# Five orders and their banks written anew, and 24 more unread products

## The reference, cut to what matters

```
mod = (silu(c) @ wmod) -> sa, ca, ga, sb, cb, gb       # per batch, per layer
# layer 0
h = layernorm(x) * (1 + ca) + sa
q, k, v = h @ w_qkv.T ; q, k = elu + 1                 # 16 heads of 8
x = x + ga * ((q @ (k^T v)) / (q @ sum k) @ w_proj.T + b)
h = layernorm(x) * (1 + cb) + sb
x = x + gb * sum over the top 2 of 8 experts: gate * (gelu(h' @ W1 + b1) @ W2 + b2)   # 128 -> 512 -> 128
# layer 1
h = layernorm(x) * (1 + ca) + sa
x = x + ga * softmax(q k^T / 4) v                      # 8 heads of 16, v 128 wide, heads summed
h = layernorm(x) * (1 + cb) + sb
x = x + gb * (h + expert_w[argmax] @ h)                # top 1 of 8
```

## Time and profile before

| | us |
|---|---|
| three runs, median | 690.94 |
| lowest, highest | 690.84, 691.75 |
| the profiled execution | 690.36 |
| its span | 688.6 |
| PE busy | 603.1 (88%) |
| DVE busy | 481.5 (70%) |
| ACT busy | 390.5 (57%) |
| POOL busy | 334.4 (49%) |
| mean granted clock of PE | 0.965 |

### The profile page before, as it was taken

The page is one execution under the profiler, slowest core; times in us unless marked ns, Lnnn a source line. Parts: engine busy times, 40 slices in busy tenths (PEclk is TensorE's granted clock), DMA queues, the critical chain, the costliest instruction groups (busy, mean ns, idle before and its releaser), DMA issues. The chain is left out here.

```text
span 688.6 us, 11893 instructions
## 1 busy us (share of the span) xinstructions
PE 603.1 (88%) x3825; PEld 386.9 (56%) x3825; DVE 481.5 (70%) x1213; ACT 390.5 (57%) x866; POOL 334.4 (49%) x363
## 2 busy tenths in 40 slices
PE   7988996999899888678998999988889897999875
PEld 4656555988798787566426498632243424533232
DVE  5277885456374654478866862896999773889996
ACT  2543043697676656336887766767665565664420
POOL 5222185447347863552773441454756273157423
PEclk9998998999999989989999999999999999999997
DMA  8200124577589688497637687216130627411121
GB/s 337 105 0 1 58 113 153 169 250 239 206 259 343 200 293 271 125 319 227 230 117 209 202 286 245 86 41 178 54 70 1 176 76 189 150 47 35 28 61 31
DMA packets 47037, 106.40 MB, mean 155 GB/s; under 512 B 7056, under 2 KB 22224, under 8 KB 45440
## 3 DMA queue, kind: packets, MB, share of 16 engines
q1 hardware_dynamic: 41424, 94.82, 43.4%
q0 software_dynamic: 5120, 10.50, 4.9%
q10 hardware_dynamic: 432, 0.34, 0.2%
HBM read 80.26 MB, written 25.17 MB: 153 GB/s over the span
## 5 line engine op out<-in xcount | busy, mean ns | idle before, releaser
L894 ACT ACTIVATE bufa<-PS 128x512 f32<-128x512 f32 x256 | 139.4, 599 | 75.2 <-PE PS L1563 68.8
L1205 DVE TENSOR_REDUCE mxs<-PS 128x2 f32<-128x1024 f32 x128 | 151.1, 1219 | 32.1 <-PE PS L1547 31.4
L853 ACT ACTIVATE bufb<-PS,bufb 128x128 f32<-128x128 f32 x368 | 103.3, 380 | 45.0 <-PE PS L1512 44.7
L1512 PE MATMUL PS<-bufb 128*128 128x128 f32 x736 | 97.5, 281 | 14.2 <-DMA bufb<-in_experts_dram 8.4
L1512 PEld LDWEIGHTS PS<-bufb 128*128 128x128 f32 x736 | 91.0, 196 | 21.0 <-issue 9.8
L1520 PE MATMUL PS<-bufb 128*128 128x128 f32 x736 | 96.3, 279 | 0.7 <-ACT bufb L853 0.6
L693 POOL DMA_INDIRECT slots_in<-bufb x64 | 67.5, 1055 | 56.4 <-DVE bufb L1151 38.3
L706 POOL DMA_INDIRECT bufb<-slots_out,bufb x64 | 61.7, 963 | 67.9 <-DMA bufb<-slots_out,bufb 35.5
L1520 PEld LDWEIGHTS PS<-bufb 128*128 128x128 f32 x736 | 90.1, 195 | 4.2 <-ACT bufb L853 1.4
L1547 PE MATMUL PS<-stk 96*128 96x512 bf16 x256 | 74.7, 384 | 15.1 <-DVE mxs L1205 5.3
L1563 PE MATMUL PS<-stk 108*128 108x512 bf16 x256 | 80.8, 387 | 7.9 <-ACT bufa L894 6.8
(11 more groups left out here) (291 smaller groups left out, 968.8 us busy)
## 6 DMA issues: line engine op xcount, KB each, us to landing
bufb<-in_experts_dram SPq DMA_DIRECT2D x92, 514.0 KB, 4.8
stk<-split SPq DMA_DIRECT2D x48, 256.0 KB, 5.2
slots_out<-bufb SPq DMA_DIRECT2D x30, 256.0 KB, 4.1
bufb<-slots_in SPq DMA_DIRECT2D x25, 256.0 KB, 3.0
split<-terms SPq DMA_DIRECT2D x8, 768.0 KB, 3.8
slots_in<-hb SPq DMA_DIRECT2D x2, 1536.0 KB, 9.5
X<-in_x_dram SPq DMA_DIRECT2D x4, 512.0 KB, 6.5
out_dram<-X SPq DMA_DIRECT2D x6, 256.0 KB, 3.4
```

The lines of the kernel that those rows point to most:

```text
L853: last = nc.scalar.activation(hs[:, n % HR, fc, :], ps[:, P * fc:P * fc + P], ACT.Gelu_apprx_tanh, bias=ws[:, n % WR, F + fc:F + fc + 1])
L894: nc.scalar.activation(probs[:, i % PR, j, :], psum("s2", i, j), ACT.Exp, scale=DH1 ** -0.5)\
L1205: nc.vector.tensor_reduce(mxs[:, gr % 2, 2 * j:2 * j + 2, h], psum("s1", i, j).rearrange("p (c n) -> p c n", c=2), axis=AX.X, op=ALU.max)\
L1512: last = nc.tensor.matmul(ps[:, P * fc:P * fc + P], ws[:, n % WR, P * fc:P * fc + P], xq[:, q % 2, P * x:P * x + P], start=True, stop=True)
```

## The change

Only the five texts of ORDERS are changed. In PE's 801 items at least 253 stand elsewhere (by 14 places at most), in ACT's 499 at least 131, in DVE's 332 at least 60, in POOL's 95 at least 15, in SP's 183 at least 47. Of 669 items with a bank 347 have another. The unread products in the loop go from 170 at 21 items to 194 at 33: two new ones at each of anm.3.1, bh.1.11, bxt.1.4, bh.2.0, bh.2.2, ctr.0.0, bh.2.5, bxt.2.2, bh.2.7, cpv.0.0, s1.1.0 and mt.0.0 ("~5"); the old ones keep their counts. ldv.0.0 moves by 76 places and is nothing still. The lines that the prediction speaks of, cut:

```diff
 "PE"
-        pc.0.0@0 atr.0.0@1 pm.0.0@0~38 aq.0.0@0~18 akv.0.0@1 akv.0.1@0 akx.0.0@0~31 anm.0.0@1~5 anm.0.1@0 aot.0.0@1~23
+        pc.0.0@1 pm.0.0@1~38 atr.0.0@1 aq.0.0@0~18 akv.0.0@1 akv.0.1@0 akx.0.0@1~31 anm.0.0@1~5 anm.0.1@0 aot.0.0@0~23
...
-        bh.1.21@2 bh.1.22@1 by.1.20@2 bxt.2.0@0 by.1.21 bxt.2.1@1 bh.2.0@0 by.1.22 btr.3.0@1 bh.2.1@0 by.2.0@1 bh.2.2@2 bh.2.3@0
-        by.2.1 ctr.0.0@0 bh.2.4@2 by.2.2 by.2.3 blg.3.0@1 bh.2.5@2 bh.2.6@0 bxt.2.2@2 by.2.4@1 by.2.5 bh.2.7@2 cpq.0.0@0
-        bh.2.8@0 bh.2.9@2~7 by.2.6 by.2.7 cpv.0.0@1 bxt.2.3@1 bh.2.10@2 bgt.3.0@0 by.2.8@1 by.2.9 bh.2.11@0 bh.2.12@2 by.2.10
-        bh.2.13@0 by.2.11 bgb.3.0@0 cpq.1.0@1 bh.2.14@1 bh.2.15@2 by.2.12@0 cpv.1.0@0 by.2.13 by.2.14 s1.0.0@0 s1.0.1@1
+        by.1.19 by.1.20@0 by.1.21 by.1.22 bxt.2.0@2 bh.2.0@2~5 bh.2.1@1 bh.2.2@2~5 ctr.0.0@0~5 bxt.2.1@0 by.2.0@2 btr.3.0@1
+        bh.2.3@1 by.2.1 by.2.2 by.2.3 bh.2.4@1 bh.2.5@1~5 cpq.0.0@1 bh.2.6@0 bxt.2.2@2~5 bh.2.7@0~5 by.2.4@2 blg.3.0@0
+        bh.2.8@0 cpv.0.0@0~5 by.2.5 by.2.6 bh.2.9@0~7 bh.2.10@1 by.2.7 cpq.1.0@0 bxt.2.3@0 bgt.3.0@2 by.2.8@1 by.2.9
+        by.2.10 bh.2.11@0 bh.2.12@2 bgb.3.0@1 by.2.11 by.2.12@0 bh.2.13@1 bh.2.14@2 bh.2.15@1 by.2.13 by.2.14 bxt.2.4@1
+        bxt.2.5@2 s1.0.0@0 cpv.1.0@1 by.2.15 s1.0.1@0 s1.1.0@0~5 bh.2.16@1 s1.1.1@1 bh.2.17@0 bh.2.18@1 s1.2.0@0 by.2.16@0
 "ACT"
-        atr.0.0 aw.0.0 aw.1.0 pm.0.0 aw.2.0 aq.0.0 akv.0.0 akv.0.1 aot.0.0 pm.0.1 aw.3.0 pm.1.0 pm.1.1 aw.4.0 pr.0.0 atr.1.0
+        aw.0.0 pm.0.0 atr.0.0 aw.1.0 aq.0.0 akv.0.0 aw.2.0 akv.0.1 aot.0.0 pm.0.1 pm.1.0 aw.3.0 aw.4.0 atr.1.0 pm.1.1
...
-        bxt.2.0 bh.2.0 by.1.5 bxt.2.1 bh.2.1 btr.3.0 bh.2.2 bh.2.3 ctr.0.0 bh.2.4 by.2.0 bh.2.5 bxt.2.2 bh.2.6 bh.2.7 cpq.0.0
-        blg.3.0 by.2.1 bh.2.9 bxt.2.3 bh.2.8 bgt.3.0 bh.2.10 bh.2.11 bh.2.12 bh.2.13 by.2.2 cpq.1.0 bh.2.14 bh.2.15 bxt.2.4
+        bh.1.18 bh.1.19 bh.1.17 bh.1.20 bh.1.21 bh.1.22 bxt.2.0 by.1.4 by.1.5 bh.2.0 bh.2.1 bh.2.2 bxt.2.1 bh.2.3
+        btr.3.0 bh.2.4 by.2.0 ctr.0.0 bh.2.6 bh.2.5 bxt.2.2 bh.2.7 cpq.0.0 blg.3.0 bh.2.8 by.2.1 bh.2.9 bh.2.10 cpq.1.0
+        bgt.3.0 bxt.2.3 bh.2.11 bh.2.12 by.2.2 bh.2.13 bh.2.14 bh.2.15 bxt.2.4 bxt.2.5 by.2.3 bh.2.16 bh.2.17 bh.2.18
 "DVE"
-        an1.0.0 an2.0.0 pc.0.0 an1.1.0 aph.0.0 apk.0.0 apk.0.1 akx.0.0 anm.0.0 anm.0.1 apr.0.0 bn1.0.0 an2.1.0 bn2.0.0 bn3.0.0
-        aph.1.0 bn4.0.0 apk.1.0 apk.1.1 an1.2.0 akx.1.0 blm.0.0 anm.1.0 anm.1.1 blg.0.0 bgt.0.0 brk.0.0 apr.1.0 bn1.1.0 an2.2.0
-        bn4.3.0 cn3.0.0 cn4.0.0 bcm.1.0 blm.3.0 blg.3.0 bgt.3.0 cpv.0.0 cpq.0.0 bcm.1.2 bcm.1.1 bcm.1.3 bcb.1.0 cn1.1.0 bgb.3.0
-        mx.15.1 bcm.2.1 msp.3.0 bcm.2.2 cpv.3.0 mtc.3.0 mx.16.0 mx.16.1 bcm.2.3 mx.17.1 bcb.2.0 cn1.2.0 mx.17.0 mx.18.0 mx.18.1
-        ds.2.0 dl2.3.0 rds.1.0 dll.3.0 fil.3.1 dx.3.0 en1.0.1 dy.3.1 dl2.3.1 dx.3.2 dy.3.3 dll.3.1 ds.3.0 dx.3.4 dy.3.5 dx.3.6
+        an1.0.0 pc.0.0 an2.0.0 an1.1.0 aph.0.0 apk.0.0 apk.0.1 akx.0.0 anm.0.0 anm.0.1 apr.0.0 bn1.0.0 an2.1.0 bn2.0.0
+        bn3.0.0 aph.1.0 an1.2.0 bn4.0.0 apk.1.0 apk.1.1 akx.1.0 blm.0.0 anm.1.0 anm.1.1 blg.0.0 bgt.0.0 brk.0.0 apr.1.0
+        cn1.0.0 bn2.3.0 bn3.3.0 bgb.2.0 cn2.0.0 cn3.0.0 bn4.3.0 cn4.0.0 cpq.0.0 blm.3.0 cpv.0.0 blg.3.0 bgt.3.0 bcm.1.0
+        mtc.2.0 mx.12.0 mx.12.1 mx.13.0 cpq.3.0 mx.13.1 mx.14.0 mx.14.1 mx.15.0 mx.15.1 msp.3.0 bcm.2.0 cpv.3.0 mtc.3.0
+        mx.16.0 bcm.2.1 bcm.2.2 mx.16.1 mx.17.0 mx.17.1 bcm.2.3 bcb.2.0 cn1.2.0 mx.18.0 mx.19.0 mx.18.1 cn2.2.0 mx.19.1
+        dx.3.0 en1.0.1 dy.3.1 dl2.3.1 dx.3.2 dy.3.3 dll.3.1 dx.3.4 dy.3.5 dx.3.6 ds.3.0 dy.3.7 ds.3.1""",
 "POOL"
-        bsc.2.2 cn1.0.0 bsc.2.3 bn3.3.0 cn2.0.0 cn3.0.0 bga.1.0 bga.1.1 bga.1.2 bga.1.3 cpt.0.0 cn1.1.0 cn2.1.0 cn3.1.0 cpt.1.0
-        rsc.0.1 rsc.0.2 cpt.7.0 rsc.0.3 fin.2.0 dn1.2.0 rga.0.0 rga.0.1 rga.0.2 rga.0.3 dx.2.0 dx.2.2 dx.2.4 dx.2.6 en1.0.0
+        bn1.3.0 bsc.2.1 bsc.2.2 bsc.2.3 cn1.0.0 bn3.3.0 cn2.0.0 cn3.0.0 bga.1.0 bga.1.1 bga.1.2 cpt.0.0 bga.1.3 cn1.1.0
+        dx.2.0 dx.2.2 dx.2.4 dx.2.6 rga.0.3 en1.0.0 dx.3.0 en1.0.1 dx.3.2 dx.3.4 dx.3.6""",
 "SP"
-        byo.0.2 byo.0.3 bw.0.22 bw.1.0 bw.1.1 byo.0.4 byo.0.5 bxl.1.0 bxl.1.1 bxl.1.2 bw.1.2 bxl.1.3 bxl.1.4 bw.1.3 bw.1.4
-        bw.2.14 cto.0.0 bw.2.15 cst.0.0 bxl.2.4 bxl.2.5 bw.2.16 bw.2.17 bw.2.18 byo.2.1 bw.2.19 bw.2.20 bw.2.21 byo.2.2 cto.1.0
+        bw.0.21 byo.0.2 bw.0.22 bxl.1.0 bxl.1.1 bxl.1.2 bw.1.0 bw.1.1 byo.0.3 byo.0.4 byo.0.5 bw.1.2 bxl.1.3 bw.1.3
+        bxl.2.4 bxl.2.5 bw.2.10 bw.2.11 cto.0.0 bw.2.12 bw.2.13 bw.2.14 bw.2.15 byo.2.0 byo.2.1 cst.0.0 bw.2.16 bw.2.17
```

More of the change, by code:

```diff
@@ L73 @@
[L73 to L81, removed]
@@ L86 @@
[L86 to L94, removed]
@@ L95 @@
[L95 to L111, removed]
-        s2.32.1@1 s2.32.2@0 fin.1.0@1 s2.32.3@0 s2.33.0@2 s2.33.1@1 ctr.3.0@1 s2.33.2@1 fin.1.1@0 pv.8.0 s2.33.3@0 s1.37.1@1
@@ new lines @@
+        pc.0.0@1 pm.0.0@1~38 atr.0.0@1 aq.0.0@0~18 akv.0.0@1 akv.0.1@0 akx.0.0@1~31 anm.0.0@1~5 anm.0.1@0 aot.0.0@0~23
+        apr.0.0@0~10 pm.0.1@1 pm.1.0@1 pm.1.1@1~9 atr.1.0@0~17 aq.1.0@0~18 pr.0.0@1~9 akv.1.0@0 akv.1.1@1 btr.0.0@1~15
+        akx.1.0@0~6 blg.0.0@1 anm.1.0@0 anm.1.1@1 aot.1.0@1~23 brk.0.0@0~30 apr.1.0@1 atr.2.0@1~90 aq.2.0@0~18 bgt.0.0@1
+        akv.2.0@1 akv.2.1@0 bgb.0.0@0 akx.2.0@0~22 anm.2.0@1~5 anm.2.1@0 bxt.0.0@0~15 aot.2.0@1 bh.0.0@1 bh.0.1@2
+        bxt.0.1@1 bh.0.2@2 apr.2.0@1 btr.1.0@0 bh.0.3@0 by.0.0@1 by.0.1 by.0.2 bh.0.4@0 blg.1.0@0 bxt.0.2@2 by.0.3
@@ new lines @@
+        atr.3.0@1 bh.0.5@0 by.0.4@2 bh.0.6@1 bh.0.7@0 bh.0.8@1 by.0.5 by.0.6 by.0.7 bxt.0.3@0 bh.0.9@0 aq.3.0@0
+        bh.0.10@2 bh.0.11@0 brk.1.0@1 bxt.0.4@2 bgt.1.0@0 by.0.8@1 by.0.9 by.0.10 by.0.11 bh.0.12@0 bh.0.13@2 bgb.1.0@0
+        bh.0.14@0 bh.0.15@1 by.0.12@2 bh.0.16@0 bh.0.17@1 by.0.13 by.0.14 by.0.15 bxt.0.5@2 bh.0.18@0 akv.3.0@0
+        by.0.16@0 akv.3.1@1 bh.0.19@2 bh.0.20@1 akx.3.0@0 by.0.17 bh.0.21@1 bh.0.22@2 by.0.18 by.0.19 by.0.20@0 by.0.21
+        by.0.22 anm.3.0@1 anm.3.1@1~5 bxt.1.0@0 bxt.1.1@2 btr.2.0@0 bh.1.0@2 blg.2.0@0 bh.1.1@0 aot.3.0@0 bh.1.2@2
@@ new lines @@
+        pv.3.1 s2.14.2@2 s2.14.3@1 s2.15.0@0 s1.18.0@0 s1.18.1@1 s2.15.1@2 s2.15.2@1 s2.15.3@0 pv.3.2 bh.3.4@1 bh.3.5@0
+        s1.19.0@0 pv.3.3 bh.3.6@2 bh.3.7@1 s1.19.1@1 bh.3.8@0 by.3.4@2 by.3.5 bxt.3.3@0 s1.20.0@0 by.3.6 s1.20.1@1
+        by.3.7 bh.3.9@1 s1.21.0@0 s1.21.1@1 by.3.8@2 bh.3.10@0 by.3.9 bh.3.11@1 mt.4.0@1 by.3.10 s1.22.0@1 bh.3.12@0
+        ctr.2.0@0 by.3.11 bh.3.13@1 cpq.4.0@0 bh.3.14@0 bh.3.15@2 by.3.12@1 by.3.13 s1.22.1@1 bxt.3.4@0 bxt.3.5@2
+        by.3.14 by.3.15 bh.3.16@2 bh.3.17@0 s1.23.0@1 cpq.5.0@0 by.3.16@0 bh.3.18@2 bh.3.19@1 by.3.17 bh.3.20@2
@@ new lines @@
+    "POOL": """
+        an1.0.0 anx.0.0 an1.1.0 bn1.0.0 bn3.0.0 anx.1.0 an1.2.0 bsc.0.0 bn1.1.0 bsc.0.1 bsc.0.2 bsc.0.3 bn3.1.0 anx.2.0
+        an1.3.0 pk.0.0 bn1.2.0 anx.3.0 bsc.1.0 bsc.1.1 bsc.1.2 bsc.1.3 bn3.2.0 bga.0.0 bga.0.1 bga.0.2 bsc.2.0 bga.0.3
+        bn1.3.0 bsc.2.1 bsc.2.2 bsc.2.3 cn1.0.0 bn3.3.0 cn2.0.0 cn3.0.0 bga.1.0 bga.1.1 bga.1.2 cpt.0.0 bga.1.3 cn1.1.0
+        cpt.1.0 cn2.1.0 cn3.1.0 bsc.3.0 bsc.3.1 bsc.3.2 bsc.3.3 bga.2.0 cpt.2.0 bga.2.1 bga.2.2 cpt.3.0 bga.2.3 cn1.2.0
+        cn2.2.0 cn3.2.0 cpt.4.0 bga.3.0 bga.3.1 bga.3.2 bga.3.3 cpt.5.0 cn1.3.0 fin.0.0 cn2.3.0 cn3.3.0 dn1.0.0 dmo.0.0
+        fin.1.0 dn1.1.0 dmo.1.0 cpt.6.0 rsc.0.0 rsc.0.1 rsc.0.2 cpt.7.0 rsc.0.3 fin.2.0 dn1.2.0 rga.0.0 rga.0.1 rga.0.2
+        dx.2.0 dx.2.2 dx.2.4 dx.2.6 rga.0.3 en1.0.0 dx.3.0 en1.0.1 dx.3.2 dx.3.4 dx.3.6""",
```

200 lines of the change are left out of this document (111 added, 89 removed).

## The result

The changed kernel takes 716.92 us (median of 4 runs, 711.65 to 719.77) where the kernel before takes 690.89 (686.50 to 691.75): a ratio of 1.038, interval 1.031 to 1.046. That is 26 us slower and not 5 us faster, 31 us above the forecast of 685.5 and outside its range of 678 to 693. Its profiled execution, the slowest of the four, took 719.77 us with a span of 718.0.

A forecast was written before the change was run, and what follows sets the result against it. It took TensorE and its waits to bound the early stages, TensorE and VectorE in turn the second half. Terms summed to −7.0, cut to −5.0 for overlap: 690.36 to 685.4, taken as 685.5 us; range 678 to 693.

The forecast's parts named there:

- Part 7: Whole kernel: 24 more unread products cost +0.8 us (0 to 5.3); banks and other moves 0, bounds ±2.
- Rival C: Unread products keep no clock, since waits of several us remain, and only delay what follows: about 688.5 us; chance 0.10.
- Part 1: Opening: modulations go first, aq.0.0 starts 3.2 us earlier; net −1.0 us at the first scatter, bounds −2.5 and 0.
- Part 2: Loads of pair 1: TensorE's 1.79 us idle at 184.32 goes as bxl.1.0 is issued earlier; −1.8 us, or 0.
- Part 3: 235 to 256 us: 4.59 us of idle becomes about 7 at ctr.0.0; sum 0, bounds −3 and +6.
- It decides when ctr.0.0 starts after about 256: Sign that the kernel turns slower: ctr.0.0, at 254.50 in the kernel before, starts after about 256 us.
- Rival E: Slower: TensorE waits 10 us and more at ctr.0.0 with all of pair 2 behind it; 694 us; chance 0.18.
- Part 4: 265 to 303 us: split terms cast and stored earlier, shortening ScalarE's and TensorE's waits; −3.5 us, bounds −6.5 and 0.
- Part 5: 375 us: TensorE's 2.35 us idle for cpv.3.0 goes, and its low clock; −3 us, bounds −3.5 and −1.
- Part 6: The end: ds.3.0 behind dx.3.6 costs +1.2 us (0 to +1.4), rga.0.3 behind dx.2.6 +0.3 (0 to +2).
- The early gain of −5.0: Whole kernel: terms sum to −7.0 us; of 2.8 from opening and loads only 0.8 is kept, giving −5.0.
- rival D: Attention from 435 us: DVE and TensorE both near full, so the early gain is swallowed; about 690.5 us; chance 0.12.

The follow-up runs named there:

- rebank: The changed kernel with only its bank numbers dealt anew, each item taking the bank whose last reader is done first by trace: 699.58 us, 1.013 of the kernel before.
- rebanknopads: rebank without the 24 new unread products: 1.009 of the kernel before.
- beforerebank: The kernel before, orders and products kept, with its banks dealt anew by the same rule from its own trace: 0.991 of the kernel before.
- tight: The kernel before with 26 bank numbers of the attention's second score products set to their predecessor's bank, no item moved: 710.69 us, 1.028 of the kernel before.
- after: The changed kernel itself, all five orders, banks and unread products as in the change: 716.92 us, 1.038 of the kernel before.
- mix: rebank's text without the new unread products up to 298 us, then orders and banks of the kernel before: 0.998 of the kernel before.
- nopads: The changed kernel without its 24 new unread products: 713.68 us, 1.032 of the kernel before.
- open112: beforerebank with the changed kernel's opening (all that starts before 112 us, banks by the rule, no new products): 685.90 us, 0.990 of the kernel before.
- open180: beforerebank with the changed orders up to 180 us, the first pair's experts included: 1.001 of the kernel before.
- tailds: rebank with ds.3.0 before dx.3.4 on VectorE again, one execution: 30.61 us from dx.3.0's first matmul to the end, against 33.82 in rebank.
- tailpool: rebank with GpSimd's last 13 items in the order of before, one execution: 29.92 us from dx.3.0's first matmul to the end, against 33.82 in rebank.
- late350: beforerebank for all that starts before 350 us, laterebank's changed orders behind, banks by the rule throughout: 1.012 of the kernel before.
- late440: beforerebank for all that starts before 440 us, laterebank's changed orders behind, banks by the rule throughout: 1.003 of the kernel before.
- laterebank: Orders of the kernel before up to 302 us, the changed kernel's behind, with banks dealt anew by the rule: 1.012 of the kernel before.
- late: Orders, banks and products of the kernel before up to 302 us, those of the changed kernel behind: 1.029 of the kernel before.

## Why the prediction was wrong

**Part 7, the banks.** This is the step that failed. "Banks and the other moves I take at 0, bounds ±2": 347 new numbers went in at nothing, priced by one wait that is no bank's. They cost 17 us against numbers dealt by the rule (rebank), and 10 or 11 if the 6 us that the rule gains on the kernel before too are taken off. The same words put all other moves of orders at 0, and these cost 12 or 13 us at like banks (rebanknopads against beforerebank). The diff alone could have told of the banks: count the items whose bank is that of the item right ahead of them. The kernel before has 10, the changed one 36, tight 37, rebank 5, beforerebank 1. (Products down, by, count here with the bank of their group.) In a line such as "s2.0.0@2 s2.0.1@2" the second must wait until ScalarE has read the first. Three of the waits in the changed kernel's trace, at bxt.0.1 (behind bh.0.0, both on bank 1), at bh.1.11 (behind bh.1.10) and at s2.0.1:

```profile
115.97 1.10 PE L1513 MATMUL PS<-identf,bufb 128*128 128x128 f32 x4 [2.87 <-ACT bufb L861]
```

```profile
220.19 1.16 PE L1520 MATMUL PS<-bufb 128*128 128x128 f32 x8 [0.80 <-ACT bufb L861]
```

```profile
335.33 0.60 PE L1571 MATMUL PS<-stk 108*128 108x512 bf16 x2 [2.03 <-ACT bufa L902]
```

Two of these are among the longest, and not all of their length is the bank's. ScalarE first loads a table (1.28 us) at s2.0.1, as it does at bh.0.0 ahead of the 2.87:

```profile
333.38 1.28 ACT L902 ACT_TABLE_LOAD   x1 [2.65 <-PE PS L1571]
```

In rebank s2.0.1 has its own bank and doesn't wait, but s2.0.2 follows at once on the bank of s2.0.0 and waits for the same exponential:

```profile
317.59 0.39 PE L1572 MATMUL PS<-stk 108*128 108x512 bf16 x1 [1.81 <-ACT bufa L903]
```

So there the new number moved the wait by one item and took 0.2 us off it. The kernel before, which had brk.3.0 and s1.5.0 between s2.0.1 and s2.0.2, waits at neither. Likewise bh.0.1 waits 2.10 us in the kernel before, for ScalarE's copy of the transposed tokens, where the changed kernel waits 2.87 at bxt.0.1. Most of the cost is in the many waits of 0.7 us.

The unread products of "bh.1.11@1~5" stand ahead of just such a wait, and hide there; at most of the other items they don't. I took +0.8 for them, near the lower bound; three pairs of runs give some 3 to 4, nearer to the upper bound of 5.3. Rival C had that mechanism right, at the right size, and 28 us too low in all.

**Part 1, the opening.** Right in mechanism and, with the banks dealt anew, in size. Rebank:

```profile
18.05 1.96 PE L1440 MATMUL PS<-xTa,wa 128*128 128x512 f32 x4 [0.67 <-ACT xTa L803]
```

aq.0.0 at 18.05 against 18.0 forecast. In the changed kernel pc, pm and atr follow each other on one pair of banks, and it starts at 19.59, behind an extra wait of 1.10 us for ScalarE's copy of pm.0.0:

```profile
16.32 1.09 PE L1432 MATMUL PS<-identf,bufa 128*128 128x128 f32 x8 [1.10 <-ACT modb L792]
...
19.59 1.95 PE L1439 MATMUL PS<-xTa,wa 128*128 128x512 f32 x4 [0.67 <-ACT xTa L802]
```

The gain behind the scatters is larger than the net −1.0 forecast and than its bound of −2.5: the eight traces with the changed opening beside after's own (rebank, mix, rebanknopads, nopads, open112, open180, tailds, tailpool) begin bh.0.0 at 105.9 to 110.7, the ten with the old opening at 109.3 to 114.7; the means lie some 4 us apart, which one trace alone could not have shown.

**Part 2.** The wait for pair 1's load is gone: after has at bxt.1.0 0.7 us for ScalarE instead of 1.79 for the DMA.

**Part 3, ctr.0.0.** Too dark. I had TensorE wait 7 us there, and it doesn't wait at all in rebank (1.2 and 1.4 us in rebanknopads and mix):

```profile
246.68 1.06 PE L1535 MATMUL PS<-identf,Hb 128*128 128x128 f32 x8
```

```profile
240.63 2.13 DVE L998 TENSOR_SCALAR bufb<-wa,mom,rstd 128x128 f32<-128x128 f32 x8
...
244.40 2.14 DVE L998 TENSOR_SCALAR Hb<-Hb,mom,rstd 128x128 f32<-128x128 f32 x8 [1.64 <-POOL rstd L677]
```

bn4.3.0 takes 2.13 us where it took 6.27, as the prediction had it once it stands apart from GpSimd's two wide operations, and cn4.0.0 ends at 246.5, four us before my 250.7, since the whole chain of pair 2's scatters began earlier (the last one at 227.51 instead of 237.82). That TensorE comes to ctr.0.0 just then, at 246.7 and not at 243.7, is chance: it had waited 1.80 and 1.17 us for the weights of bh.2.0 and bh.2.1, a wait that I had not in the sum. "It decides when ctr.0.0 starts after about 256": in the changed kernel it does, with only 2.29 us of wait:

```profile
258.96 1.55 PE L1534 MATMUL PS<-identf,Hb 128*128 128x128 f32 x8 [2.29 <-DVE Hb L997]
```

Rival E's sign and its threshold came true, and its mechanism did not; TensorE was late before it got there.

**Part 4.** Right in the waits. ScalarE's wait at cpq.1.0 is 0.62 us in rebank (0.55 in after) instead of 9.63, bh.2.15's 7.42 is gone in both, and in rebank s1.0.0 starts at 294.50, 8.2 us ahead (in the changed kernel, late by then, at 310.5):

```profile
276.27 1.27 ACT L889 ACTIVATE terms<-PS,cols 128x512 bf16<-128x512 f32 x2 [0.62 <-DMA split<-terms]
...
294.50 0.59 PE L1556 MATMUL PS<-stk 96*128 96x512 bf16 x2 [3.22 <-DMA stk<-split]
```

A wait of 3.22 us for the loads of stk has taken the place of 0.97, so even here the next in line shows.

The terms were ready at 270 and not at 277, as GpSimd's gathers for bga.1.2 began at 262.09 instead of 273.74. But the 8.2 are not the price of these orders, and don't show that my −3.5 was too small. The traces with the new orders and banks by the rule (rebank, rebanknopads, mix, tailds, tailpool) are ahead at s1.0.0 by 2.6 to 8.2 us, 6.1 in the mean; the six with the old orders and banks by the rule by 2.5 to 7.2, 4.5 in the mean, though some of them still wait 5.0 to 7.7 us at bh.2.15. What the early orders bring by 300 us is within the spread of the traces.

**Part 5.** The 2.35 us at 375 are gone in after and in rebank, where s1.16.0 waits for nothing. It shows nowhere in the time: rebank's lead shrinks up to there, and late350 against late440 leaves up to 0.9% of loss to the changed orders from 350 to 440 us. Which of their items make it was not tried.

**Part 6.** In the changed kernel ds.3.0 stands fully in VectorE's last chain, without the gap that covered it in the earlier trace rows:

```profile
708.12 0.68 DVE L1355 TENSOR_TENSOR bufb<-bufb,modb 128x512 f32<-128x512 f32 x1
708.84 1.63 DVE L1356 TENSOR_TENSOR X<-X,bufb 128x512 f32<-128x512 f32 x1
710.39 0.60 DVE L1337 TENSOR_SCALAR bufb<-PS,bufb 128x128 f32<-128x128 f32 x2
```

Its second instruction takes 1.63 us there instead of 0.69, beside an addition of dx.3.6 on GpSimd (1.64 us from 708.28). ds.3.0 costs 1.65 us instead of 1.2; the order of GpSimd 0.6, or 2.2 with the slow spell, instead of 0.3: 2.3 to 3.9 us instead of 1.5. I had looked at rga.0.3 there; dx.3.0 ahead of en1.0.1 is the likelier half, since rga.0.3 ends 11 us before dx.3.0 in the trace, but tailpool took both back.

**The sum.** The early gain of −5.0 is not there as a gain of the orders: at s1.0.0 they are worth 1.6 us in the means above. And rival D holds for it at the end, where open112 is level with beforerebank (0.990 and 0.991), rebanknopads with laterebank (1.009 and 1.012) and mix with the kernel before (0.998). It doesn't hold for banks: beforerebank's 0.9% does arrive. In the traces leads melt on the way. Beforerebank is 2.5 us ahead at s1.0.0 and 0.4 at s1.52.0, open112 4.4 and 2.8, mix 2.3 at s1.40.0 and none at s1.52.0. One place where it goes is this row of beforerebank, at s1.52.0:

```profile
582.40 1.86 PE L1556 MATMUL PS<-stk 96*128 96x512 bf16 x4 [4.05 <-DMA stk<-split]
```

It is 2.09 us in the kernel before: the terms of the last batch's scores come through cpt.7.0, which GpSimd does behind three scatters, and through two DMAs, and who is early waits there. Of the 26 us that the change costs, in terms of the runs: banks 17, products 3 to 4, and the rest, 6, is the new orders of the attention and the end less what the early ones gain. So the 31 us between the forecast and the measurement are banks 17 for 0, orders +6 for −5.8, and products 3 to 4 for 0.8. This division holds against the kernel before as it is; had that had its banks by the rule, the orders would be charged with 12 or 13 and the banks with 10 or 11. Which moves of the attention make the orders' part was not found.

My 0.2% for what one measurement tells was too little as well: nineteen executions of the kernel before on one chip lay between 684.41 and 698.53 us.

## What to carry to other kernels

Where an order written by hand names the buffers too, read the two as one text: for each item ask who had its bank before, how far back that stands, and in which place of the reader's order. A bank number cost little here where several items lay between, and where none did 0.7 us as a rule and 2 to 3 where the reader had a table to load first; 26 such numbers were 2.8%. And price a change of many small moves at its spread, not at nothing: seven stalls found and removed by name were worth less than the 347 numbers that I had not read.

## What the runs showed that I had not expected

- Dealing the banks of the tuned kernel anew by one rule (take the bank whose last reader is done first by the trace) gains 0.9%, with no item moved.
- A wait of 2.79 us in place of 1.64 was followed by matmuls at the lower clock (3.54 instead of 1.98 us for four) in rebank and not in laterebank, and twelve matmuls behind one and the same order of TensorE took 7.09 us in rebank and 5.40 in late.
- Five kernels with one text up to 350 us reach the first expert tile within a range of 4.6 us (109.3 to 113.9), so a stall of one or two us that a single trace shows there is not yet a price.
